# The write half of three layer norms moved from VectorE to GpSimd, a bias copy moved from ScalarE to VectorE, and both placed anew

## What is computed

```
h = layernorm(x) * (1 + ca) + sa                     # norm 0
x1 = x + ga * attention_16_heads_causal(h)
h2 = layernorm(x1) * (1 + cb) + sb                   # norm 1, then scale and shift
xn = layernorm(h2) * ln_g + ln_b                     # norm 2
o  = attention_32_heads(xn) + h2
y  = experts(o)        # 8 experts, two per batch: gelu(o @ w1 + b1) @ w2 + b2
out = x1 + gb * y
```

## Time and profile before

| | |
|---|---|
| median of 3 runs (lowest to highest) | 1814.58 us (1813.31 to 1815.22) |
| the profiled execution: its own time, its span | 1813.31 us, 1811.6 us |
| one turn of the loop | about 201 us, six of them |
| busy share of the span | TensorE 83%, VectorE 64%, ScalarE 56%, GpSimd 30% |

### The profile page before, as it was taken

One profiled execution on the slowest core, in us unless ns is written; L12 is line 12 of the kernel. 1 busy time (PEld: TensorE's weight loads), 2 busy tenths in 40 slices (PEclk: granted clock), 3 DMA queues, 4 the chain that ended last, 5 costly groups with the idle time before them and its releaser, 6 DMA issues.

```text
span 1811.6 us, 30221 instructions
## 1 busy us (share of the span) xinstructions
PE 1510.7 (83%) x10001; PEld 660.3 (36%) x10001; DVE 1157.0 (64%) x2957; ACT 1006.1 (56%) x2095; POOL 537.7 (30%) x1253
## 2 busy tenths in 40 slices
PE   4476677998899988998899988998899897879777
PEld 2232222334433353334433353334433352324315
DVE  3265628975598647975597648964697638775440
ACT  0034243675467645775467655774567645666572
POOL 1232433422243313422243313522252314300100
PEclk8578787999999999999999999999999999999999
DMA  6533032342333523442433523432423423121301
GB/s 178 142 101 82 21 111 80 112 111 83 96 105 100 133 74 106 120 98 80 127 85 86 132 74 114 133 95 63 143 86 92 110 74 103 63 51 45 111 2 58
DMA packets 137269, 171.25 MB, mean 95 GB/s; under 512 B 16984, under 2 KB 102808, under 8 KB 137120
## 3 DMA queue, kind: packets, MB, share of 16 engines
q1 hardware_dynamic: 137120, 169.33, 33.9%
HBM read 110.67 MB, written 56.66 MB: 92 GB/s over the span
## 4 chain that ended last, share of the span: by engine, by line
PE 64%; DVE 16%; ACT 8%; issue 5%; DMA 3%; SPq 2%; POOL 1%; POOLq 0%; ACTq 0%; DVEq 0%
PE bank_out L1109 15%; PE bank_scores L1092 10%; DVE neg_max L1289 8%; PE bank_max L1063 8%; PE bank_side L1196 6%; PE bank_side L1030 6%; ACT probs L883 4%; PE bank_side L1040 4%; PE bank_side L1180 3%; PE bank_scores L1180 3%; PE bank_side L1118 2%; DVE normed L1248 2%; PE bank_side L1152 2%; PE bank_side L1161 2%; DMA q_stack<-max_parts 1%
## 5 line engine op out<-in xcount | busy, mean ns | idle before, releaser
L883 ACT ACTIVATE probs<-bank_scores 128x512 f32<-128x512 f32 (+3 forms) x1536 | 753.3, 545 | 476.7 <-PE bank_scores L1092 467.7
L1289 DVE TENSOR_REDUCE neg_max<-bank_max 128x1 f32<-128x512 f32 x1024 | 653.6, 682 | 169.9 <-PE bank_max L1063 165.1
L1092 PE MATMUL bank_scores<-q_stack,k_stack 64*128 64x512 bf16 (+3 forms) x2048 | 320.4, 349 | 94.3 <-ACT probs L883 73.6
L1063 PE MATMUL bank_max<-k_stack,q_stack 64*128 64x512 bf16 (+3 forms) x2048 | 321.7, 350 | 86.0 <-DVE neg_max L1289 46.4
L1109 PE MATMUL bank_out<-probs,v_tile 128*9 128x512 f32 (+4 forms) x3072 | 370.1, 554 | 15.5 <-ACT out_raw L897 12.3
L1286 DVE CUSTOM_DVE_ANT_0 bank_max<-bank_max,causal 128x384 f32<-128x384 f32 (+3 forms) x512 | 241.7, 514 | 108.5 <-PE bank_max L1063 106.6
L1092 PEld LDWEIGHTS bank_scores<-q_stack,k_stack 64*128 64x128 bf16 x2048 | 85.5, 94 | 369.9 <-issue 342.0
L770 POOL TENSOR_SCALAR_AFFINE_SELECT probs<-probs 128x512 f32<-128x512 f32 x128 | 81.0, 633 | 353.1 <-ACT probs L883 353.0
L1063 PEld LDWEIGHTS bank_max<-k_stack,q_stack 64*128 64x128 bf16 x2048 | 106.6, 95 | 175.2 <-issue 103.0
L752 POOL CAST max_parts<-max_row 16x128 bf16<-16x128 f32 x96 | 28.4, 296 | 385.9 <-DVE max_row L1300 385.9
L1196 PE MATMUL bank_side<-w_out,hidden_T 128*128 128x256 f32 x512 | 118.8, 385 | 4.7 <-issue 3.7
(11 more groups left out here) (116 smaller groups left out, 1513.6 us busy)
## 6 DMA issues: line engine op xcount, KB each, us to landing
q_stack<-q_parts SPq DMA_DIRECT2D x128, 256.0 KB, 4.3
k_stack<-k_parts SPq DMA_DIRECT2D x128, 192.0 KB, 6.0
w_in<-in_L_ffn_w_dram SPq DMA_DIRECT2D x16, 1024.0 KB, 5.6
w_out<-in_L_ffn_w_dram SPq DMA_DIRECT2D x16, 1024.0 KB, 8.5
q_parts<-partsq SPq DMA_DIRECT2D x32, 384.0 KB, 2.6
k_parts<-partsk SPq DMA_DIRECT2D x32, 384.0 KB, 2.6
q_parts<-partsq SPq DMA_DIRECT2D x32, 256.0 KB, 2.9
k_parts<-partsk SPq DMA_DIRECT2D x32, 256.0 KB, 2.9
```

The source lines that it names most:

```text
L883: nc.scalar.activation(probs[s % 2][:, head_at(k), q0:S], region[bank][:, q0:S], ACT.Exp, scale=float(WIDTH[a]) ** -0.5).then_inc(drained[ ...
L1063: ins = pe.matmul(region[to][:, 0:keys], q_stack[buf][rows, at, qt * P:(qt + 1) * P], k_stack[buf][rows, at, 0:keys], start=(i == 0), stop ...
L1092: ins = pe.matmul(region[to][:, q0:S], k_stack[buf][rows, at, kt * P:(kt + 1) * P], q_stack[buf][rows, at, q0:S], start=(i == 0), stop=last)
L1289: v.tensor_reduce(dst, region[bank], AX_X, ALU.max).then_inc(drained[bank], 1)
```

## The change

Pieces 7 and 8 of every norm are done by GpSimd instead of VectorE. GpSimd waits for the last Newton step and, before it overwrites `normed`, for the TensorE transposes that read the tile before. `bias_columns` is done by VectorE instead of ScalarE, and waits there for the batch before to be finished (`y_made`). The placing of all norms but the first two changes; in the loop norm 0 takes slots 12 to 28 instead of 8 to 25 with its `to_features` on 29 and 33 instead of 31 and 33, norm 1 takes 30 to 54 instead of 34 to 54, and norm 2 takes 70 to 86 instead of 70 to 87.

```diff
-def place_norm(plan, ats, off, n):
-    place_at(plan, ats, layernorm_items(off, n))
+def place_layernorm(plan, at, off, n, together=1):
+    for piece, item in enumerate(layernorm_items(off, n)):
+        place(plan, at + piece // together, [item])
...
@@ before
-    place_norm(beside, (82, 82, 83, 83, 83, 83, 83, 84, 85), 0, 1)
-    place(beside, 86, [("ffn_input", 0, 0), ("ffn_input", 0, 1), ("load_mod", 1)])
+    place_layernorm(beside, 82, 0, 1, 2)
+    place(beside, 87, [("ffn_input", 0, 0), ("ffn_input", 0, 1), ("load_mod", 1)])
     place(beside, 93, features_items(0, 1))
-    place_norm(beside, (89, 89, 90, 90, 90, 90, 90, 91, 92), 0, 2)
+    place_layernorm(beside, 90, 0, 2, 2)
...
@@ loop
-    place_norm(beside, (8, 10, 12, 14, 14, 14, 15, 24, 25), 2, 0)
+    place(beside, 12, layernorm_items(2, 0), 2)
-    place_at(beside, (31, 33), features_items(2, 0))
+    place_at(beside, (29, 33), features_items(2, 0))
-    place_norm(beside, (34, 36, 38, 40, 41, 42, 42, 52, 54), 1, 1)
-    place_at(beside, (55, 60, 60), [("ffn_input", 1, 0), ("ffn_input", 1, 1), ("load_mod", 2)])
+    place(beside, 30, layernorm_items(1, 1), 3)
+    place(beside, 60, [("ffn_input", 1, 0), ("ffn_input", 1, 1), ("load_mod", 2)])
-    place_norm(beside, (70, 72, 74, 76, 76, 77, 77, 86, 87), 1, 2)
+    place(beside, 70, layernorm_items(1, 2), 2)
...
@@ after
-    place_norm(beside, (24, 25, 26, 27, 27, 27, 27, 30, 31), 1, 1)
+    place_layernorm(beside, 24, 1, 1)
-    place_norm(beside, (43, 44, 45, 46, 46, 46, 46, 50, 51), 1, 2)
+    place_layernorm(beside, 44, 1, 2)
...
@@ GpSimd
             def layernorm(b, f, n, piece):
+                src = (x_in, x1, ffn_x)[n]
+                dst = normed[n % 2]
...
+                half = piece - NEWTON_PIECE - 1
+                if half == 0:
+                    wait(pool, rstd_made[n], ROOT_STEPS * (b + 1))
+                    for user in ((0, 2), (1,), (0, 2))[n]:
+                        if user in turned_fill:
+                            bank, _ = turned_fill[user]
+                            wait(pool, filled[bank], number(turned_fill[user]) + 1)
+                for t in range(2 * half, 2 * half + 2):
+                    pool.tensor_scalar(dst[:, t, :], src[:, t, :], mean_var[:, n, t, 0:1], rstd[:, n, t:t + 1],
+                                       ALU.subtract, ALU.mult).then_inc(normed_made[n], 1)
...
@@ ScalarE
-            def bias_columns(b, f):
-                for j in range(2):
-                    e = (b * 2 + j) % E
-                    nc.scalar.activation(b1_cur[:, j, :], b1_T[:, e * FT:(e + 1) * FT], ACT.Copy).then_inc(b1_made, 1)
...
@@ VectorE
-                    for t in range(2 * half, 2 * half + 2):
-                        v.tensor_scalar(dst[:, t, :], src[:, t, :], mean_var[:, n, t, 0:1], rstd[:, n, t:t + 1],
-                                        ALU.subtract, ALU.mult).then_inc(normed_made[n], 1)
...
+            def bias_columns(b, f):
+                if b > 0:
+                    wait(dve, y_made, 2 * b + 1)
+                for j in range(2):
+                    v.tensor_copy(b1_cur[:, j, :], b1_T[:, (b * 2 + j) % E * FT:((b * 2 + j) % E + 1) * FT]).then_inc(b1_made, 1)
```

More of the change, by code:

```diff
@@ L808, in bias_part, with to_features @@
                         pool.tensor_tensor(x_res[:, t, :], x1[:, t, :], b2_bc[:, j, :], ALU.add).then_inc(res_made, 1)
+            turned_fill = {}
+            def to_features(b, f, n, cc):
+                turned_fill[n] = f[0]
             def layernorm(b, f, n, piece):
+                src = (x_in, x1, ffn_x)[n]
+                dst = normed[n % 2]
+                if piece < NEWTON_PIECE:
+                    return
                 if piece == NEWTON_PIECE:
@@ L832, in _ @@
             walk(pool, {"layernorm": layernorm}, start=True)
-            walk(pool, {"layernorm": layernorm, "qk": qk, "max_rows": max_rows, "scores": scores, "ffn_input": ffn_input, "bias_part": bias_part,
+            walk(pool, {"layernorm": layernorm, "to_features": to_features, "qk": qk, "max_rows": max_rows, "scores": scores, "ffn_input": ffn_input, "bias_part": bias_part,
                         "attention_out": attention_out, "expert_out": expert_out})
@@ L946, in keep_x @@
                 nc.scalar.activation(ffn_xT[:, :, :], ffn_xT_next[:, :, :], ACT.Copy).then_inc(x_kept, 1)
-            walk(act, {"bias_columns": bias_columns, "keep_v": keep_v, "keep_x": keep_x, "ffn_sum": ffn_sum,
+            walk(act, {"keep_v": keep_v, "keep_x": keep_x, "ffn_sum": ffn_sum,
                        "qk": qk, "v": v, "to_features": to_features, "scores": scores, "sums_out": sums_out,
@@ L1241, in layernorm @@
                     first_guess(b, n, piece - 3)
[L1242 to L1245, removed]
-                    dst = normed[n % 2]
-                    for t in range(2 * half, 2 * half + 2):
-                        v.tensor_scalar(dst[:, t, :], src[:, t, :], mean_var[:, n, t, 0:1], rstd[:, n, t:t + 1],
-                                        ALU.subtract, ALU.mult).then_inc(normed_made[n], 1)
             def to_features(b, f, n, cc):
@@ L1390, in _ @@
                        "max_rows": max_rows, "normalise": normalise, "attention_out": attention_out,
-                       "ffn_sum": ffn_sum, "expert_out": expert_out})
+                       "bias_columns": bias_columns, "ffn_sum": ffn_sum, "expert_out": expert_out})
 _INS = ["L0_attn_in_features", "L0_attn_q_proj_weight", "L0_attn_k_proj_weight", "L0_attn_v_proj_weight",
```

## The result

The changed kernel takes 1890.79 us (median of 4 runs, 1889.06 to 1892.87) against 1814.9 us for the kernel before (4 runs): ratio 1.042, 95% interval 1.0401 to 1.0438. It is 76 us slower; 5.5 us less were forecast, and the time lies far above the range of 1795 to 1822. Every ratio in this document compares a kernel with the kernel before measured again beside it, whose medians were 1812.9 to 1818.8 us; so where two experiments are compared, their ratios count for more than their medians.

What follows compares the result with a forecast made beforehand. TensorE and VectorE were both taken as full where the norms lie. Loop -3.6, before it -1.5, after it -0.4 make -5.5 against 1813.31: 1807.8; with 1.3 for the median, 1809 us, range 1795 to 1822.

Steps and rivals of the forecast that it cites:

- Moving the write relieves VectorE by about 3 us a turn: Three norms of a loop turn: VectorE's queue gets 3 x 1.3 = 3.9 us shorter; full relief would gain 3.0.
- A write takes 440 ns, with 396 and 729 as bounds: Each normed write on GpSimd: 440 ns, between a one-input copy's 396 and a two-input instruction's 729.
- Norm 0: In the loop: late Newton and writes make TensorE wait 2.35 us before its transposes; net +1.2 us a turn.
- Norm 2: In the loop: writes end at 778.8, just before TensorE wants them at 779.1; -0.8 us a turn.
- The section before the loop: Before the loop: transposes of norm 2 begin at about 222.2 instead of 223.68, -1.5 us.
- the prediction's own sum: Loop: 1.2 - 1.0 - 0.8 = -0.6 us a turn, -3.6 us in six turns.
- Norm 1: In the loop: TensorE's waits behind VectorE's normed go, -1.0 us a turn; no wait over 0.3 us for GpSimd's write.
- The bias copy costs 0, at most +1 us: Slot 8: 16 copies of 0.1 to 0.2 us on VectorE while TensorE waits for max parts; cost 0, at most +1.
- TensorE's clock: Whole kernel: the sum had no term for a lower clock; the norms' windows were read at full clock.
- The slots: New loop places: last guess directly before the fourth attention_out, Newton behind its residual add; charged at norm 0, +1.2 us a turn.
- The section after the loop: After the loop: a 3.07 us wait goes, but late scores take most of it back; net -0.4 us, 0 to -3.
- the costly write: Rival, chance 0.14: a GpSimd write takes 729 ns, total 1824; the loop's sum turns positive from about 550 ns.

Runs made afterwards that it cites:

- The price list: Kernel before plus eight forms of GpSimd instruction, four each, behind all other work; mean times: copy 400 ns, one constant 856, two scalars per partition 1224.
- the one with the writes hidden: Kernel before with the loop's normed writes on GpSimd, 4 to 7 slots earlier; VectorE writes outside the loop: 1797.01 us, ratio 0.9918.
- the plain copy: Changed kernel with a plain one-input copy in place of each normalising write on GpSimd, normalisation left out: 1833.37 us, ratio 1.0092.

## Why the prediction was wrong, step by step

**Moving the write relieves VectorE by about 3 us a turn:** right. 2.85 us, where nothing was given back.

**A write takes 440 ns, with 396 and 729 as bounds: the first term that failed.** It takes 1220 ns. I reckoned it from its number of tensor inputs and from the slope of the mask, 0.81 ns a column. The price list shows 3.3 ns a column for this form. The four-element row (222 ns) that I began from is a form with one constant, and even that form takes 856 ns at 256 columns, (856 - 222) / 252 = 2.5 ns a column. So the slope was the mistake: neither the mask nor the number of tensor inputs tells it. A copy of that tile takes 400 ns, the form with two scalars per partition 1224; which part of the form makes the difference stays open.

**The places and their mechanism:** right, and this can be worked out. With 1.22 for 0.44, four writes end 4 x 0.78 = 3.1 us later. Norm 0: a stop of 2.35 + 3.1 = 5.5; measured 5.52. Norm 2: writes end at 778.8 + 3.1 = 781.9, wanted at 779.1, a stop of 2.8; measured 3.07. The section before the loop: -1.5 + 8 x 0.78 = +4.7; measured 303.1 - 298.3 = +4.8, though that agreement is of sums alone and closer than this stage repeats from kernel to kernel (3.6 us with the same plan). In the loop the prediction's own sum would have been 1.2 + 3.1 - 1.0 - 0.8 + 2.8 = +5.3 us a turn. Norm 1 had no wait for the write, as forecast.

**The bias copy costs 0, at most +1 us: the second term that failed.** 23 us alone, 11 to 13 within the changed kernel. I priced the instruction at 0.1 to 0.2 us, which it takes on slot 14 (0.16), and named a transfer of max parts as its cover at slot 8. The kernel before waits 0.30 us for max parts there, far less than the 2.1 us that a copy took. And on slot 7 `bias_part` stands directly ahead of it in the plan, and its six GpSimd instructions run just then; the change put a VectorE copy beside them.

**TensorE's clock:** not in the sum, nor among the rivals. Taking the rows of one turn against the same forms at full clock: behind norm 0, from 754.70 to 760.4, 5.9 us of work instead of 3.9; behind norm 2, from 813.64 to 817.9, 4.7 instead of 3.1. That is 3.6 us a turn, an estimate from two places of one turn. Over all six turns the same matmuls took 18.8 us longer than before, 3.1 a turn. The clock is a cost that the sum put at nothing without a reason, the third term that failed.

**The turn put together:** 5.3 for the write, 3.6 for the clock, 1.7 for the bias copy (211.87 - 210.18) make 10.6; measured 10.24. By the windows of the loop, idle time makes 7.1 of it and slower matmuls 3.1; the reckoned idle time is 5.3 + 1.7 = 7.0. Six turns are 61 us of the 76.

**The slots:** I charged them with the order at norm 0 only. Alone they cost 41 us; within the change, putting norm 0's back gives 25 to 28. With a cheap write on GpSimd they do no harm (1812.21). With the 1.22 us write they leave it no time, and with VectorE's write the maxima queue behind it. The slots of norm 2 are not to blame: its stop is 3.07 or 3.08 us on the old slots and on the new ones.

**The section after the loop** cost 9.1 us instead of -0.4. Alone the bias copy makes 6.6 there and the slots 13.5 (in an execution 12.6 above its median), the write nothing. One wait of 6.2 us for the write stands in it, and the waits for max parts grew from 7.2 to 12.7 us; how these add up stays open, also because this stage differed by 3.2 us between two kernels with the same plan in it.

**The rivals:** the costly write had the right side and the right mechanism. It was priced at a two-input instruction as the far end, so it came out at 1824 instead of 1890.8, and it had no slow clock either. Its threshold of 550 ns follows from the prediction's terms; no run tried a price between 400 and 1220 ns. The Trainium skill (GPSIMD Engine Reference, Engine selection) sorts by the number of inputs; the measured form has one and is slower than the two-input form, 1224 against 613 ns here, so the page's split doesn't hold for it. Its advice to keep elementwise work on VectorE was right for this plan, and not for the one with the writes hidden.

## What to carry to other kernels

Price an instruction by a row of its own form and size: here a form with one tensor input cost twice what one with two did, and where no row has the form, the upper bound is open and not the dearest row at hand. A slow engine is free as long as its work ends before it is asked for: the same writes on GpSimd cost 2.25 us a turn on the old slots, and moved a few slots forward they gained 2.85; move the place with the work. And when an instruction changes engine, look at what the neighbouring engine does in that same slot, and count a stop of TensorE at more than its own length.

## What the runs showed of the hardware that I had not expected

- GpSimd, fp32, 128x256: copy 400 ns; two constants 407; one constant 856; one scalar per partition 922, two 1224.
- A VectorE copy of 128x8 took 162 ns where GpSimd ran nothing beside it and up to 2.1 us while GpSimd ran additions back to back.
- TensorE's granted clock fell to 1.2 GHz behind stops in the middle of a busy stretch, and stayed there for some 3 to 5 us behind those of 2.40, 3.07 and 5.52 us shown above. Behind the two longest this cost 1.6 and 2.0 us beside the stop itself.
- The length of the stop alone didn't settle it. In the loops of the 13 kernels of the table the clock fell, during the stop or within about 2 us behind it, at none of the 12 stops of 1.03 us, at 9 of 16 of about 1.74 us, at 38 of 42 of 3.07 to 3.19 us, and at all 18 of 5.5 us and more. Behind the stop of 2.06 us shown (the plain copy, third turn) it stayed at 2.4 GHz; behind the other four such stops of that kernel, and behind all five of the same kernel with the bias on ScalarE, it fell. One of these five, at 727.43:

```profile
727.40:731.40 4.00, 3.63 (x16) 1.23 (x20) 2.70 (x6) 1.98 (x4) 0.00 (x0) 0.50 0.00 0
```
